# An adaptive-norm attention and expert block: eight scatters of normed rows, sent one by one around the first inverse deviation

## The reference

```python
h = _layernorm(x, axis=-1) * (1 + ca) + sa
x = x + ga * _L0_attn_ref(h, ...)
h = _layernorm(x, axis=-1) * (1 + cb) + sb
x = x + gb * _L0_ffn_ref(h, ...)
# in the attention
out = jnp.einsum('bhnd,bhde->bhne', q, state)
out = (out - mu) * jax.lax.rsqrt(var + 1e-05) * ln_g + ln_b
out = out @ Wo.T + bo
# in the feed-forward: two experts of eight for each row, and a shared one
scores = jax.nn.sigmoid(xf @ gate_w + bias)
top_scores, top_idx = jax.lax.top_k(scores, K)
out = (shared + combined)
out = out / (jnp.max(jnp.abs(out), axis=-1, keepdims=True) + 1e-06)
```

## Time and profile before

| | us |
|---|---|
| time before, median of 3 runs (912.34 to 914.35) | 913.25 |
| profiled execution, its span | 937.9 |
| TensorE busy in the span | 855.0 (91%) |
| VectorE busy | 634.0 (68%) |
| ScalarE busy | 474.3 (51%) |
| GpSimd busy | 401.5 (43%) |

### The profile page before, as it was taken

One profiled execution on the slowest core, in us unless ns is written; L12 is line 12 of the kernel. 1 busy time (PEld: TensorE's weight loads), 2 busy tenths in 40 slices (PEclk: granted clock), 3 DMA queues, 4 the chain that ended last, 5 costly groups with the idle time before them and its releaser, 6 DMA issues. The chain is left out here.

```text
span 937.9 us, 21404 instructions
## 1 busy us (share of the span) xinstructions
PE 855.0 (91%) x5989; PEld 783.1 (83%) x5990; DVE 634.0 (68%) x1675; ACT 474.3 (51%) x880; POOL 401.5 (43%) x415
## 2 busy tenths in 40 slices
PE   6999999899989889999889999989999999999970
PEld 5778878788878768788779999979999999999970
DVE  5789986659777677687766666566666565566651
ACT  3766554254433543544556555545555554455530
POOL 3643500304232251352502655555656565565563
PEclk9999999889999999999989999999999999999986
DMA  8120000922232241240661332253334333444442
GB/s 285 65 90 1 1 1 1 269 52 58 67 107 41 76 116 25 90 115 13 240 227 49 94 94 76 76 166 85 90 66 95 80 91 84 89 87 82 78 82 48
DMA packets 68609, 83.31 MB, mean 89 GB/s; under 512 B 23088, under 2 KB 56842, under 8 KB 68400
## 3 DMA queue, kind: packets, MB, share of 16 engines
q0 software_dynamic: 25792, 39.92, 18.3%
q1 hardware_dynamic: 41920, 41.64, 14.2%
q10 hardware_dynamic: 816, 0.79, 0.3%
HBM read 45.44 MB, written 41.55 MB: 93 GB/s over the span
## 5 line engine op out<-in xcount | busy, mean ns | idle before, releaser
L1847 PE MATMUL psUp<-eT,wup 128*128 128x256 f32 x1632 | 205.8, 286 | 10.9 <-issue 7.9
L1847 PEld LDWEIGHTS psUp<-eT,wup 128*128 128x128 f32 x1632 | 199.4, 192 | 16.1 <-issue 13.6
L1873 PE MATMUL psY<-wdn,gTh 128*128 128x256 f32 x1088 | 200.9, 286 | 1.0 <-issue 1.0
L1873 PEld LDWEIGHTS psY<-wdn,gTh 128*128 128x128 f32 x1088 | 169.7, 192 | 0.6 <-issue 0.6
L1873 PE MATMUL psY<-wdn,gTl 128*128 128x256 f32 x544 | 154.2, 283 | 0.0
L1930 ACT ACTIVATE ys<-yc,meta 128x256 f32<-128x256 f32 x68 | 30.9, 502 | 182.6 <-DVE yc L1997 146.3
L2120 POOL DMA_INDIRECT out<-fin,oidx x68 | 109.4, 1609 | 22.8 <-issue 17.4
L1911 ACT ACTIVATE gu<-psUp,ubias 128x256 f32<-128x256 f32 x272 | 113.5, 469 | 7.7 <-PE psUp L1847 3.9
L1976 DVE TENSOR_TENSOR gTl<-gu,gTh 128x512 fp32r<-128x512 f32 x136 | 93.7, 689 | 32.6 <-ACT gTh L1916 23.4
L2110 POOL DMA_INDIRECT shared_part<-ys,widx x68 | 70.5, 1037 | 97.4 <-ACT ys L1930 56.9
L1173 PE MATMUL psY<-sd,ghi 128*128 128x256 f32 x512 | 97.6, 289 | 11.5 <-DVE glo L1399 11.4
(11 more groups left out here) (297 smaller groups left out, 1439.9 us busy)
## 6 DMA issues: line engine op xcount, KB each, us to landing
hin<-expert_in SPq DMA_DIRECT2D x36, 256.0 KB
X<-in_L_attn_x SPq DMA_DIRECT2D x8, 512.0 KB, 7.4
X<-bo_row POOLq DMA_DIRECT2D x8, 512.0 KB
shared_part<-prow SPq DMA_DIRECT2D x8, 512.0 KB, 6.3
shared_part<-sh SPq DMA_DIRECT2D x8, 512.0 KB
out<-X SPq DMA_DIRECT2D x8, 512.0 KB
raw_up<-in_L_ffn_up_w SPq DMA_DIRECT2D x3, 1024.0 KB
raw_dn<-in_L_ffn_down_w SPq DMA_DIRECT2D x3, 1024.0 KB, 9.5
```

Of the source, the lines that this page charges most:

```text
L1847: mm = nc.tensor.matmul(psU[:, c, (m % 2) * TR:(m % 2 + 1) * TR], wup[s][:, a, k, m * P:(m + 1) * P], eT[:, u, b, k], start=(n == 0), stop ...
L1873: mm = nc.tensor.matmul(psE[:, u, h * C:(h + 1) * C], (gTh, gTl)[a][:, u, m, h * P:(h + 1) * P], wdn[s][:, b, m], start=(n == 0), stop=(n ...
```

## The change

`scatter` gets the block, the buffer, the tiles and a switch as arguments. In the bodies 2 to 7 the scatters of block g - 2 now stand at the head of body g instead of at the end of body g - 1: those of the tiles 0 and 1 (four DMAs) ahead of `rstd(0)`, those of the tiles 2 and 3 between `rstd(0)` and `rstd(1)`. Each of them but the very first waits until the one ahead has landed. Body 8 sends the scatters of the blocks 6 and 7 as before, eight in a row each, without such waits.

```diff
-                def scatter():
+                def scatter(f, r, tiles, one_by_one):
                     if isinstance(f, int) and f == 0:
                         pool.wait_ge(pad_st, 16 * E)
                     wait(pool, pos_ok, f + 1)
-                    for t in range(TG):
+                    for t in tiles:
                         for k in range(TOPK):
+                            n = t * TOPK + k
+                            if one_by_one and (later(f, 1) or n):
+                                wait(pool, scat, 16 * (TG * TOPK * f + n))
                             nc.gpsimd.indirect_dma_start(
...
-                if att_on:
-                    if isinstance(g, int) and g == 0:
-                        bias(0)
-                    rstd(0)
-                    rstd(1)
-                if att_on and not (isinstance(g, int) and g == NG - 1):
-                    bias(g + 1)
-                if ffn_on:
-                    scatter()
+                if not att_on:
+                    scatter(f - 1, q, range(TG), False)
+                    scatter(f, r, range(TG), False)
+                    return
+                if isinstance(g, int) and g == 0:
+                    bias(0)
+                if later(g, 2):
+                    scatter(f - 1, q, (0, 1), True)
+                rstd(0)
+                if later(g, 2):
+                    scatter(f - 1, q, (2, 3), True)
+                rstd(1)
+                if not (isinstance(g, int) and g == NG - 1):
+                    bias(g + 1)
```

## The result

| | us |
|---|---|
| before, median of 5 runs beside it (909.81 to 914.35) | 912.34 |
| after, median of 5 runs (915.41 to 917.97) | 916.31 |
| after, profiled execution, its span | 914.4 |

The ratio is 1.0047, with a 95% interval of 1.0031 to 1.0063: 4.0 us are lost. The profiled execution of after agrees with its times. That of before, with 937.9 us, doesn't, so totals of the two pages can't be subtracted. What follows reads after by itself, and then beside profiles of other kernels.

The account below looks back on a forecast made before the run. TensorE was taken to bound the attention stage, with GpSimd a bound in block 7 alone. 1.35 us there plus 3 x 0.4 us in blocks 4 to 6 made 2.55, added to 913.25: 915.8 us, range 909.5 to 919.5.

Parts of the forecast that it names:

- The price of a wait: GpSimd's scatters waiting one by one: about 3.25 us from issue to issue, ends 2.4 and 3.75, against 1.30 in the burst.
- The fourth scatter: Block 4, ahead of the first deviation: third scatter held behind SyncE's store to about 310.0, fourth starts at 311.4.
- Block 7: Third scatter 0.71 us behind the store, fourth at 421.4, line 1354 1.8 us late, 0.43 covered: 1.35 us of loss.
- Blocks 4 to 6: First deviation late behind the held scatter; TensorE loses 0 to 0.8 us, taken as 0.4 in each block.
- Blocks 2 and 3: Third scatter lands before the stores; in block 3 the fourth ends 10.7 us behind the first: no loss.
- The second four: Scatters behind the first deviation, block 7: eighth over at 435.4, second deviation wanted at 435.8, just covered, 0.4 us spare.
- Block 1 as one that stores nothing: Attention stage: block 1, said to store nothing, keeps TensorE busy 34.29 of 35.83 us, read as TensorE bounding the stage.
- sharing with the store packet by packet (B): Rival, chance 0.25: third scatter takes turns with the store's packets and passes with little delay; nothing is late, 913.3 us.
- B's other way: Same rival, chance 0.25 in all: a wait costs 2.4 us, third scatter issued at 304.6 ahead of the store, 913.3 us.
- the faster one (C): Rival, chance 0.15: fewer scatters beside the stores shrink VectorE's remote waits; 909.0 us for half, 904.7 for all.
- the remote waits of line 1339 gone: Sign for the faster rival: VectorE's four waits for a release filed under "remote", 11.0 us, disappear from the attention stage.
- The late second four (D): Rival, chance 0.10: at 3.75 us a step the eighth scatter delays the second deviation, 4.4 us more over blocks 4 to 7, 920.2.

Follow-up runs that it names:

- undisturbed profile: The kernel before, unchanged, profiled a second time: 911.66 us, its span 909.8, no remote wait.
- Three ahead and five behind: The changed kernel with three scatters ahead of the first inverse deviation and five behind it, instead of four and four: 916.98 us, ratio 1.0043.
- written-out run: The changed kernel with GpSimd's blocks 3 to 6 written out instead of looped over, same instruction order: 914.7 us, ratio 1.003; again 914.78 us, 1.0034.

## Why the prediction was right, and where its steps were not

The forecast was 915.8 us, slower, and the time is 916.3. The mechanism is the one that it named: the third scatter issued behind SyncE's store, held, the first deviation late at line 1354, TensorE waiting at line 1089. The terms were sized less well than their sum.

- *The price of a wait*, 3.25 us from issue to issue: 3.36 and 3.27 in block 4. In the written-out blocks it is 2.73, which no row of the kernel before could show; no run explains why the gather that the price was read from fits the loop, so the hit is in part luck. The bounds 2.4 and 3.75 rested on no row; the loop's form of the wait is worth 2.28 - 1.74 = 0.54 us.
- *The fourth scatter*, put at 11.6 us behind the first (311.4 - 299.78): 11.94 in block 4. Its hold was well sized, 311.4 - (299.78 + 9.75) = 1.9 us against 4.32 - 2.29 = 2.0. The parts weren't: 43 of the third's packets came through 9.1 to 9.9 us behind the first scatter, where the prediction had 10.2, and the last five later than the rest, which it didn't have.
- *Block 7*, charged 1.35 us: nothing. This step failed, because it took one price for all blocks, and 3.25 holds in the loop alone. With 2.73 the third scatter stands 5.53 us behind the first, not 6.5, and clears the store, which comes 6.39 behind. Its sign for this block, line 1354 waiting about 3 us, didn't come: the line doesn't wait there.
- *Blocks 4 to 6*, charged 0.4 each: 1.61, 0.77 and 1.35. This term was mis-sized. Both its ends, 0 and 0.8, took the remote wait as absent; they differ in how much sooner TensorE then comes, 1.84 or 2.94 us, and the middle was taken. In the undisturbed profile it comes 17.76 - 14.69 = 3.07 us sooner, counted from the first scatter, so the upper end was the right one. And 0.8 was itself too small: TensorE wants the rows 309.74 - 295.05 = 14.7 us behind the first scatter in the undisturbed profile and would have had to have them 313.50 - 1.61 - 297.53 = 14.4 behind in the changed kernel, where the prediction had 314.6 - 299.78 = 14.8 at its early end; they came at 16.0 instead of 15.6.
- *Blocks 2 and 3*, nothing: right, line 1354 waits in blocks 4 to 6 alone. But in block 3 the fourth ends 12.95 us behind the first, not 10.7, mostly because of the late landing without a store, and this happens to be covered.
- *The second four*, just covered: right. The second deviation of block 7 still waits 1.00 us for VectorE, and no reader waits for it. Three ahead and five behind shows how little spare there is.
- *Block 1 as one that stores nothing*: misread, but no term rests on it. The store of block 0's rows is issued at 233.60 us, 2.5 us ahead of the end of that stretch.

So 1.35 + 1.2 was predicted where 0 + 3.7 came: two errors of opposite sign. So it is luck in part that the time came near. It was 2.55 us added to 913.25, while 4.0 were lost on 912.34. Of the rivals, sharing with the store packet by packet (B) falls in the loop by the 113 packets that let none through; B's other way, a third scatter ahead of the store with nothing late, is what came in block 7. The sign given for the faster one (C), the remote waits of line 1339 gone, came too, but the second profile of the kernel before has none either, so C falls. The late second four (D) fall in block 7 by the 1.00 us of spare.

## What to carry to other kernels

Here a wait for a small transfer could be hidden until the transfer met a large one: place the awaited transfer ahead of the store, or leave the wait out. Before a loss is costed against a profile, compare its span with the timed runs; if it is longer, take the due times without the waits that only it can have. A spacing measured inside a hardware loop doesn't hold for the written-out blocks around it.

## What the runs showed of the hardware

- With a constant to compare with, and nothing that held the landing, a waited scatter ahead of the first deviation starts 1.72 to 1.77 us behind the end of the one ahead; in the loop, where the wait takes its value from a register and is followed by one more semaphore step, 2.27 to 2.29. The written-out run separates the loop's form from the constant's, not the register from the extra step.
- A scatter issued 1.3 us behind a store of 512 KB, with a second such store behind it, got none of its 48 packets through while the store's queue was at 98.2%, and landed some 2 us late, about 1 us of it with the last five packets.
- A scatter with no store near landed 1.6 us late (3.85 us of idle time behind it instead of 2.27 to 2.29), with one packet of 0.02 MB of the instruction queue beside its own.
- With waits of 4.0 to 5.6 us of TensorE in each of the blocks the mean granted clock of the blocks was 0.91 to 0.95, with 3.4 to 6.8 us at 1.2 GHz from late in each wait on; with waits of 0.8 to 1.6 us it stayed at 1.00, that is 2.4 GHz.
